# A gated cross-attention and MoE layer on one core: softmax maxima finished 12 half slots ahead, weighted sums at every slot's end

## The chip, the cores and the metric

The kernel runs on one core of a Trainium2 chip. The metric is the device time of one execution in microseconds (us). A core has five engines that run beside each other, each with its own program in order: PE (matmuls; PEld is its weight load), DVE (vector), ACT (activations), POOL (general purpose, also issues some DMAs) and SP (issues DMAs). They meet by semaphores only.

## The reference, cut to what matters

16 batches of 512 tokens with 256 channels, and a context of 1601 rows with 128 channels. Each batch goes through layer norm, causal self-attention and cross-attention with 16 heads of 16, a projection, a residual, and then a mixture of experts (32 experts, top 4) plus a shared expert:

```
q, k, v = heads(x @ Wq + bq), heads(x @ Wk + bk), heads(x @ Wv + bv)
att  = where(causal, q k^T * scale, -inf);  y  = softmax(att) v
attc = qc kc^T * scale;                     y += softmax(attc) vc      # 1601 context rows
x = x + tanh(g) * (y @ Wp + bp)
x = x + tanh(g2) * (top-4 experts(layernorm(x)) + shared expert)
```

A softmax needs the maximum of each row, or something near it, before the exponentials.

## The kernel before, in words

**Parts.** The attention program is written out as a prologue P, a first batch F, 14 middle batches M, a last batch L, and a remainder X (`plan`, `run` in each engine's program). Then come the experts (`build_experts`) and a merge. A batch of attention carries the next batch's loads, norm and q/k/v work, and the projection, router, shared expert and routing of the batch before it.

**Slots.** A batch has 68 slots (`SLOTS`), four quads of 17: quad g = 2*ch + v holds 4 heads, with 13 slots of 128 context rows ("cross") and 4 of 128 own rows ("self"). A slot has two half slots of two heads each, so a batch has 136 half slots, and a quad 34. PE's order in one slot is (`run` in `pe_program`): scores of pair 0, items of the first half slot, scores of pair 1, items of the second, and at one of four places the weighted sums of the slot before. ACT takes the exponential of each score tile (line 766) into `prob`, which has two buffers, one per slot; PE multiplies `prob` with the values into the one bank `outs` (line 576). In the four self slots POOL first clears what lies above the diagonal (`mask`, line 1165), and the sums wait for that.

**The ring.** Scores and items take turns in seven PSUM banks (`RB`, `ring`), strictly in order of PE's program (`Plan.claim`). PE waits before it writes a bank until its last reader has read it: ACT for scores, DVE for most items.

**Maxima.** The row maxima of a quad are taken from a separate, coarser product of 34 items (`max_items`): 8 `own`, 24 `cross`, 2 `rest`. Each has two score tiles that PE computes (lines 634, 643, 654 and 659) and DVE reduces (line 962). When all are in, DVE makes `whole` (line 968), PE turns the result (`shift`, line 667), ACT and DVE write its two bf16 rows into `mr`, and SP sends them by 4 DMAs into the operand rows of the scores (`stacks<-mr`, line 1427). Scores of the quad wait for these (`rowed`). Before the change a quad's maxima end 6 half slots ahead of its first scores (`early = 6`): `whole` at half slots 28, 62, 96 and 130.

**What sets the order.** For F and L a planner deals items at fixed places and fills maxima by costs (`deal`, `fill`), with the sums after the second half slot's items (place 3). For the 14 middle batches three tables do it: `PLACED` (half slot of each item by group), `MAXIMA` (number of maximum items in each half slot) and `SUMS_AT` (place of the sums in each slot: 0 after pair 0's scores, 1 after its items, 2 after pair 1's scores, 3 after its items). Of the items, these matter here:

- `finish_a`: the last batch's load of x (`xr`), `bias`, four `outproj`, `norm2`, two `trans`, `router`. After the last `outproj` DVE makes the statistics, POOL the inverse root in 16 small steps (`inverse_root`, lines 1152 to 1158, 4 rounds of 4), and DVE the normalised rows (`norm2`, line 888) that `trans` turns on PE. In POOL's program the second part of an item comes one half slot later, behind `mask` if that is a second half slot and ahead of it if it is a first.
- `split`: q, k and context projections in three bf16 pieces; `value`: the value projections; `stack`: SP's loads of operands, 12 DMAs each; SP stores a finished piece one half slot after it.
- `route`: the top-4 choice on DVE in 15 half slots from 77 on; `scatter`: 16 indirect DMAs of POOL. The first `split` of quad pair 1 waits on ACT until all 16 have landed (line 800).
- `divide` on POOL: products of 128x1024 and 128x512 (lines 1200 and 1204), at slots 7 and 41.

## Time and profile before

| | us |
|---|---|
| median of 3 runs | 4718.81 (4696.34 to 4723.49) |
| the profiled execution | 4715.91 |
| its span in the trace | 4713.8 |
| PE busy | 4143.5 (88%) |
| DVE busy | 3554.8 (75%) |
| ACT busy | 2678.1 (57%) |
| POOL busy | 1647.1 (35%) |

In the trace, L12 is line 12 of the kernel; `PE ring L552` is PE's instruction of that line that writes `ring`. A number in brackets behind a timeline row is the idle time of the engine before it, and what ended it. The profiled execution's time is 2.1 us more than its span, and lies 2.9 us under the median. PEclk (or the clock in a window) is the share of full speed that was granted to TensorE: it has two levels, 0.5 (1.2 GHz) and 1.0 (2.4 GHz), and a window shows their mean.

### The profile page before, as it was taken

The page shows a single profiled execution, that of the slowest core. Times are in us where ns is not written, and L with a number is a line of the kernel's source. Part 1 is how long each engine was busy: PE and PEld are TensorE (multiplying, and loading weights), DVE is VectorE, ACT ScalarE, POOL GpSimd, SP SyncE. Part 2 cuts the span into 40 slices and gives each one's busy share as a digit, 9 for nine tenths or more (in the row PEclk, how much of TensorE's full clock was granted, in tenths as well). Part 3 has the DMA queues.
Part 4 walks back from the last instruction along what each step waited for, and adds up shares of the span by engine and source line. Part 5 has one row for each costly group of instructions (what it writes and reads, how often), then busy time and mean ns, then how long its engine had stood idle before and what let it go on. Part 6 is the DMA issues. An engine that isn't in the chain of part 4 may idle for free. (4 is left out here: it accounts for less than half of the span.)

```text
span 4713.8 us, 87834 instructions
## 1 busy us (share of the span) xinstructions
PE 4143.5 (88%) x30693; PEld 1734.6 (37%) x30693; DVE 3554.8 (75%) x7733; ACT 2678.1 (57%) x5523; POOL 1647.1 (35%) x2168
## 2 busy tenths in 40 slices
PE   4999999999999999999999989999999995788882
PEld 1333333323333333333333333333333322577771
DVE  5888888888979797879797979787888873344442
ACT  1665656565656565656565666666665663444440
POOL 1122323232323232323232323223232313588883
PEclk7999999999999999999999999999999997899996
DMA  3333434343434343434343334343433335888888
GB/s 111 82 84 84 110 81 115 82 116 77 115 81 115 78 113 78 116 73 114 85 113 86 108 89 106 88 107 85 110 84 103 95 102 161 170 151 150 149 150 246
DMA packets 384060, 514.13 MB, mean 109 GB/s; under 512 B 84628, under 2 KB 248324, under 8 KB 383680
## 3 DMA queue, kind: packets, MB, share of 16 engines
q1 hardware_dynamic: 288720, 380.51, 30.5%
q0 software_dynamic: 87728, 115.39, 13.6%
q10 hardware_dynamic: 7232, 13.26, 0.9%
q8 instruction: 227, 3.72, 0.3%
q14 instruction: 153, 1.25, 0.1%
HBM read 288.49 MB, written 201.27 MB: 104 GB/s over the span
## 5 line engine op out<-in xcount | busy, mean ns | idle before, releaser
L766 ACT ACTIVATE prob<-ring 128x512 f32<-128x512 f32 (+3 forms) x4352 | 2132.9, 562 | 1185.2 <-PE ring L552 1153.3
L962 DVE TENSOR_REDUCE pmx<-ring 128x1 f32<-128x512 f32 (+1 forms) x3328 | 1992.0, 662 | 169.3 <-PE ring L634 153.2
L552 PE MATMUL ring<-stacks 64*128 64x512 bf16 (+1 forms) x8704 | 1308.3, 374 | 123.2 <-DMA stacks<-mr 56.1
L576 PE MATMUL outs<-prob,vt 128*32 128x512 f32 x8704 | 1106.3, 581 | 90.1 <-POOL prob L1165 88.3
L552 PEld LDWEIGHTS ring<-stacks 64*128 64x128 bf16 (+1 forms) x8704 | 331.9, 96 | 1169.3 <-issue 627.7
L634 PE MATMUL ring<-stacks 64*128 64x512 bf16 x3072 | 609.8, 394 | 16.2 <-DVE pmx L962 3.3
L962 DVE TENSOR_REDUCE mc<-ring 128x1 f32<-128x128 f32 (+3 forms) x1024 | 432.0, 482 | 243.6 <-PE ring L659 241.0
L1690 POOL DMA_INDIRECT scratch_sums<-e_yo,e_tok x320 | 495.9, 1550 | 117.3 <-issue 82.5
L1165 POOL TENSOR_SCALAR_AFFINE_SELECT prob<-prob 128x512 f32<-128x512 f32 x256 | 167.1, 653 | 1015.8 <-ACT prob L766 1013.7
L1235 POOL TENSOR_TENSOR split<-rest,split 128x512 bf16<-128x512 f32 (+1 forms) x224 | 218.9, 977 | 778.2 <-DVE split L1057 775.6
L1662 DVE TENSOR_SCALAR e_yo<-e_py,e_wcol 128x256 f32<-128x256 f32 x320 | 140.2, 480 | 286.8 <-DMA scratch_sums<-e_yo,e_tok 284.6
L576 PEld LDWEIGHTS outs<-prob,vt 128*32 128x32 f32 x8704 | 173.8, 109 | 472.5 <-issue 295.7
L634 PEld LDWEIGHTS ring<-stacks 64*128 64x128 bf16 x3072 | 177.4, 97 | 428.1 <-issue 130.3
L1564 PE MATMUL e_ph<-e_xt,e_we 128*128 128x256 f32 x1280 | 307.2, 383 | 3.4 <-ACT e_xt L1600 3.2
L1224 POOL DMA_INDIRECT scratch_slots<-split,rows x256 | 252.6, 987 | 92.6 <-issue 69.9
L800 ACT ACTIVATE split<-ring,bcol 128x512 bf16<-128x512 f32 (+1 forms) x224 | 142.1, 636 | 215.4 <-PE ring L603 124.3
L1609 ACT COPY e_we<-stacks 128x768 f32 x160 | 133.1, 832 | 230.9 <-issue 121.6
L1564 PEld LDWEIGHTS e_ph<-e_xt,e_we 128*128 128x128 f32 x1280 | 240.6, 191 | 45.3 <-ACT e_xt L1600 12.4
L1573 PE MATMUL e_py<-e_we,e_act 128*128 128x256 f32 x640 | 178.8, 402 | 61.5 <-DVE e_act L1646 59.5
L1054 DVE SCALAR_TENSOR_TENSOR rest<-ring,bcol,split 128x512 f32<-128x512 f32 (+1 forms) x224 | 150.9, 674 | 91.7 <-ACT split L800 91.7
L654 PE MATMUL ring<-stacks 64*128 64x128 bf16 (+3 forms) x1024 | 169.5, 331 | 46.8 <-DMA stacks<-scratch_parts 15.7
L1200 POOL TENSOR_TENSOR num<-num,den 128x1024 f32<-128x1024 f32 x31 | 73.3, 2365 | 228.7 <-DMA den<-scratch_inverses 223.1
(168 smaller groups left out, 3744.0 us busy)
## 6 DMA issues: line engine op xcount, KB each, us to landing
stacks<-scratch_parts SPq DMA_DIRECT2D x1536, 64.0 KB, 3.1
stacks<-scratch_parts SPq DMA_DIRECT2D x768, 68.1 KB, 2.6
scratch_parts<-split SPq DMA_DIRECT2D x64, 768.0 KB, 4.1
e_xin<-scratch_slots SPq DMA_DIRECT2D x160, 289.0 KB, 3.6
scratch_parts<-split SPq DMA_DIRECT2D x32, 816.8 KB, 4.3
num<-oc POOLq DMA_DIRECT2D x256, 64.0 KB
den<-scratch_inverses POOLq DMA_DIRECT2D x63, 256.0 KB, 7.7
ct<-in_ctx_t_dram SPq DMA_DIRECT2D x16, 800.5 KB, 5.2
```

The costliest lines, as they stand in the source:

```text
L552: mm = eng.matmul(dst[0:m, q0:T], kst[g][step][on, pair, k0:k0 + m], qst[g][step][on, pair, qc + q0:qc + T], start=step == 0, stop=step == 1)
L576: mm = eng.matmul(po[32 * j:32 * j + 32, q0:T], vt[ch][0:m, VW * vi + VE * hl:VW * vi + VE * hl + 32], prob[0:m, n % 2, j, q0:T], start=kt ...
L634: eng.matmul(dst, qst[g][0][on, pair, 128 * qt:128 * qt + 128], kst[g][0][on, pair, T + 512 * of:T + 512 * of + 512], start=True, stop=Tru ...
L654: eng.matmul(dsts[side][:, 0:n], qst[g][0][on, pair, T + 128 * qt:T + n], kst[g][0][on, pair, 0:n], start=True, stop=False)
L766: eng.activation(prob[0:m, n % 2, j, q0:T], pm[0:m, PLANS[part.kind].bank[i], q0:T], ACT.Exp, scale=SCALE).then_inc(exped.sem, 1)
L962: eng.tensor_reduce(dst, src, AX.X, ALU.max).then_inc(free_of(part, it, side), 1)
L1165: eng.affine_select(out=prob[:, n % 2, :, q0:q0 + 128], in_=prob[:, n % 2, :, q0:q0 + 128], compare_op=ALU.is_ge, fill=0.0, base=0, patter ...
L1224: eng.indirect_dma_start(scr["slots"], bass.IndirectOffsetOnAxis(ap=rows[:, NQ * k + q:NQ * k + q + 1].bitcast(U32), axis=0), xs[:, ROW * ...
L1235: eng.tensor_tensor(last, rest[:, no % 2, 0:n], mid, ALU.subtract).then_inc(low.sem, 1)
L1564: op = eng.matmul(phd[i][:, m, :], we[g % UW][:, c0:c0 + H], xt[i][:, kc, :], start=kc == 0, stop=kc == KC - 1)
L1573: op = eng.matmul(py[i][:, q, :], act[i][:, 128 * q:128 * q + 128], we[g % UW][:, 2 * KC * H:], start=True, stop=True)
L1690: eng.indirect_dma_start(scr[f"sums{i}"], bass.IndirectOffsetOnAxis(ap=tok[u][:, q:q + 1].bitcast(U32), axis=0), yo[g % UO][:, q, :], None ...
```

## The change

Maxima now end 12 half slots ahead of the quad's scores (`AHEAD`), so `whole` stands at half slots 22, 56, 90 and 124. The first 13 maximum items of quad 1 (8 `own`, 5 `cross`) move from a batch's start into the last 12 half slots of the batch before it (`NEXT`, items marked "next"); F does them for the first middle batch, and all 34 of its own besides; L has only the 21 that are left for quad 1. The sums stand at place 3 in every slot. The tables of the middle batches are others: with that, `outproj` moves from (26, 26, 30, 30) to (24, 26, 32, 32), `trans`, `trans`, `router` from (40, 40, 40) to (40, 42, 42), the scatters from one in each half slot from 96 on to (98, 99, 102, 102, 102, ... 111), and `stack` items go earlier. The route items stay where they were, the other places move by a few half slots. DVE's waits ahead of `whole` name the newest use of each bank instead of the quad's last items. No instruction of a middle batch is added or removed.

```diff
+AHEAD, NEXT = 12, 13
+
+
+def parted_items(q, which):
+
+    items, costs = max_items(q)
+    if which == "next":
+        return [it + ("next",) for it in items[:NEXT]], costs[:NEXT]
+    return (items[NEXT:], costs[NEXT:]) if which == "rest" else (items, costs)
+
...
 PLACED = {
-    "value1": (1, 6, 8, 8, 11),
-    "stack2": (12, 16, 20),
-    "stack3": (50, 54, 58),
-    "finish_a": (8, 24, 26, 26, 30, 30, 37, 40, 40, 40),
-    "finish_b": (44, 47),
-    "finish_c": (50, 50, 50, 51),
-    "next": (42, 54, 47, 53, 56, 56),
-    "split0": (57, 60, 62, 67, 69, 72, 73),
-    "value0": (93, 97, 100, 104, 108),
-    "split1": (114, 118, 119, 124, 126, 130, 131),
+    "value1": (2, 2, 8, 10, 10),
+    "stack2": (6, 10, 14),
+    "stack3": (44, 48, 52),
+    "finish_a": (8, 24, 24, 26, 32, 32, 37, 40, 42, 42),
+    "finish_b": (44, 45),
+    "finish_c": (50, 50, 50, 50),
+    "next": (42, 54, 47, 53, 54, 54),
+    "split0": (56, 60, 61, 67, 68, 70, 72),
+    "value0": (94, 100, 103, 107, 110),
+    "split1": (114, 118, 120, 124, 125, 128, 133),
     "route": (77, 78, 79, 80, 81, 82, 83, 84, 85, 86, 87, 89, 91, 92, 93),
-    "scatter": (96, 97, 98, 99, 100, 101, 102, 103, 104, 105, 106, 107, 108, 109, 110, 111),
-    "stack0": (84, 88, 92),
-    "stack1": (118, 122, 126),
+    "scatter": (98, 99, 102, 102, 102, 103, 105, 107, 107, 107, 108, 108, 108, 109, 111, 111),
+    "stack0": (78, 82, 86),
+    "stack1": (112, 116, 120),
 }
 MAXIMA = (
-    3, 2, 2, 1, 0, 1, 1, 2, 1, 1, 1, 2, 1, 1, 0, 1, 2, 1, 1, 1, 0, 2, 1, 1, 1, 2, 0, 2, 2, 1, 2, 0, 0, 1,
-    1, 2, 0, 0, 0, 1, 1, 2, 0, 1, 2, 1, 0, 2, 1, 2, 0, 2, 1, 0, 1, 1, 1, 2, 1, 2, 0, 1, 4, 1, 3, 0, 3, 0,
-    0, 3, 0, 2, 1, 0, 2, 1, 2, 1, 2, 0, 0, 0, 0, 0, 0, 1, 0, 0, 0, 3, 0, 1, 0, 0, 1, 3, 0, 0, 2, 1, 1, 1,
-    1, 2, 0, 1, 0, 1, 2, 1, 1, 1, 0, 1, 2, 1, 1, 1, 2, 2, 0, 1, 1, 2, 0, 0, 2, 0, 1, 2, 0, 0, 0, 0, 0, 0,
+    0, 0, 1, 2, 0, 1, 1, 1, 1, 2, 2, 2, 1, 1, 0, 2, 0, 1, 0, 2, 0, 1, 1, 0, 2, 2, 2, 2, 0, 1, 0, 1, 1, 0,
+    0, 2, 0, 0, 0, 0, 2, 1, 2, 2, 2, 2, 0, 1, 0, 1, 2, 1, 0, 1, 1, 2, 4, 1, 2, 2, 3, 1, 1, 1, 0, 1, 1, 2,
+    1, 1, 1, 1, 1, 1, 1, 1, 1, 1, 1, 0, 0, 0, 0, 0, 0, 1, 0, 0, 0, 3, 1, 1, 0, 1, 2, 2, 1, 1, 0, 1, 1, 1,
+    0, 2, 0, 1, 1, 0, 1, 1, 2, 2, 1, 1, 2, 1, 0, 1, 2, 1, 1, 1, 0, 1, 2, 1, 1, 1, 2, 0, 1, 2, 0, 1, 1, 1,
 )
 SUMS_AT = (
-    1, 1, 3, 3, 3, 1, 2, 3, 1, 3, 3, 3, 2, 3, 3, 2, 3, 0, 3, 3, 3, 3, 3, 0, 2, 3, 2, 2, 3, 2, 2, 2, 2, 1,
-    1, 2, 3, 2, 3, 1, 3, 3, 3, 1, 1, 1, 3, 2, 0, 3, 1, 2, 2, 3, 3, 2, 3, 3, 2, 1, 3, 2, 3, 2, 2, 2, 2, 2,
+    3, 3, 3, 3, 3, 3, 3, 3, 3, 3, 3, 3, 3, 3, 3, 3, 3, 3, 3, 3, 3, 3, 3, 3, 3, 3, 3, 3, 3, 3, 3, 3, 3, 3,
+    3, 3, 3, 3, 3, 3, 3, 3, 3, 3, 3, 3, 3, 3, 3, 3, 3, 3, 3, 3, 3, 3, 3, 3, 3, 3, 3, 3, 3, 3, 3, 3, 3, 3,
 )
 
 
...
                 i += 1
 
     fin, more = kind in "ML", kind in "FM"
-    quad, early = HALF // 2, 6
+    quad = HALF // 2
     deal("value1", 0, (3, 5, 7, 9, 11), value_items(1), 1.35)
-    deal("stack2", 0, (12, 16, 20), stack_items(2), 0.0)
-    deal("stack3", 0, (50, 54, 58), stack_items(3), 0.0)
+    deal("stack2", 0, (6, 10, 14), stack_items(2), 0.0)
+    deal("stack3", 0, (44, 48, 52), stack_items(3), 0.0)
     if fin:
         deal("finish_a", 0, (8, 24, 27, 27, 31, 31, 37, 39, 39, 41), FINISH[:10], 0.9)
         deal("finish_b", 0, (43, 45), FINISH[10:12], 2.9)
...
     if kind == "L":
         deal("experts", 0, (36, 70, 104), [("experts", i) for i in range(3)], 0.0)
     if more:
-        deal("stack0", 0, (84, 88, 92), stack_items(0), 0.0)
-        deal("stack1", 0, (118, 122, 126), stack_items(1), 0.0)
-    at = 0
-    for q in range(1, 5 if more else 4):
-        fill(at, quad * q - early, *max_items(q % 4))
-        at = quad * q - early
-        out[at].append(("whole", q % 4))
-        out[at + 1].append(("shift", q % 4))
+        deal("stack0", 0, (78, 82, 86), stack_items(0), 0.0)
+        deal("stack1", 0, (112, 116, 120), stack_items(1), 0.0)
+    stages = [(1, 0, quad - AHEAD, "rest" if fin else "all")]
+    stages += [(q % 4, quad * (q - 1) - AHEAD, quad * q - AHEAD, "all") for q in range(2, 5 if more else 4)]
+    if more:
+        stages.append((1, 2 * HALF - AHEAD, 2 * HALF, "next"))
+    for g, lo, hi, which in stages:
+        fill(lo, hi, *parted_items(g, which))
+        if which != "next":
+            out[hi].append(("whole", g))
+            out[hi + 1].append(("shift", g))
 
     first = {2 * n + p // 2 for n in range(SLOTS) for p in (0, 2) if sums_at(kind, n) == p}
...
+        def newest_of(part, g):
+
+            p = PLANS[part.kind]
+            mine = [it for here in p.items for it in here if it[0] in ("own", "cross", "rest") and it[1] == g and it[-1] != "next"]
+            return {p.bank[it, i]: p.turn[it, i] for it in mine for i in range(BANKS[it[0]])}
...
-        load_no = lambda part, g: 1 if part.kind == "P" else (1, 0, 1, 1)[g]
+        load_no = lambda part, it: 1 if part.kind == "P" or it[-1] == "next" else (1, 0, 1, 1)[it[1]]
...
-                    pe.wait_ge(stacked_rest[g], part, load_no(part, g))
+                    g, pair, qt, of = it[1:5]
+                    pe.wait_ge(stacked_rest[g], part, load_no(part, it))
...
-                    newest = {bank_of(part, it, i): (it, i) for it in max_items(g)[0] for i in range(BANKS[it[0]])}
-                    for last, i in newest.values():
-                        read(dve, part, last, i)
+                    for k in range(RB):
+                        dve.wait_ge(freed[k], part, newest_of(part, g).get(k, 0))
                     eng.tensor_reduce(mc[g % 2][:, :].rearrange("p (h a q) -> p h a q", a=2, q=NQ)[:, :, 0, :], pmx[:, :, :, :],
                                       AX.X, ALU.max).then_inc(whole.sem, 1)
```

## Rows read from the trace of the kernel before

**Rows 1.** The page, part 1: busy time, share of the span, instructions
```profile
PE 4143.5 (88%) x30693; PEld 1734.6 (37%) x30693; DVE 3554.8 (75%) x7733; ACT 2678.1 (57%) x5523; POOL 1647.1 (35%) x2168
```

**Rows 2.** Windows: first, middle, last batches, two single ones; length, busy, clock, DMA
```profile
116.23:335.08 218.85, 208.52 (x1670) 70.07 (x1672) 179.03 (x365) 145.09 (x301) 44.86 (x72) 0.98 0.35 84
335.08:3711.99 3376.91, 3125.03 (x24618) 1130.25 (x24615) 2837.14 (x6020) 2085.84 (x4271) 1008.28 (x1596) 0.96 0.38 97
3711.99:3924.00 212.01, 196.15 (x1548) 64.54 (x1548) 141.40 (x301) 137.65 (x286) 54.30 (x83) 0.95 0.39 105
...
577.73:820.50 242.77, 224.97 (x1764) 80.78 (x1762) 202.81 (x430) 149.07 (x305) 71.92 (x114) 0.95 0.38 96
1304.22:1542.19 237.97, 219.45 (x1763) 79.96 (x1761) 202.41 (x430) 148.95 (x306) 72.12 (x114) 0.98 0.38 98
```

**Rows 3.** Waits of PE, middle batch 1304.2:1542.2: total us, times, longest
```profile
PE outs L576 <- POOL prob L1165: 6.0, 3, 5.0
PE ring L552 <- DMA stacks<-mr: 3.8, 1, 3.8
PE ring L552 <- DVE pmx L962: 3.5, 4, 2.6
PE ring L682 <- ACT xt L789: 1.0, 1, 1.0
```

**Rows 4.** Timeline of PE around slot 16
```profile
1357.29 0.61 PE L552 MATMUL ring<-stacks 64*128 64x512 bf16 x4
1362.93 0.65 PE L576 MATMUL outs<-prob,vt 128*32 128x128 f32 x8 [5.03 <-POOL prob L1165]
```

**Rows 5.** Timeline of POOL there, first root step and mask
```profile
1357.90 0.20 POOL L1152 TENSOR_TENSOR newt<-rstd 128x4 f32<-128x4 f32 x1 [1.24 <-DVE rstd L882]
...
1362.24 0.63 POOL L1165 TENSOR_SCALAR_AFFINE_SELECT prob<-prob 128x512 f32<-128x512 f32 x1
```

**Rows 6.** Timeline of DVE, statistics and normalisation of the same batch
```profile
1355.59 1.40 DVE L874 BATCH_NORM_STATS2 stat<-ct 128x6 f32<-128x256 f32 x4
...
1368.05 1.38 DVE L888 TENSOR_SCALAR xa<-ct,mv,rstd 128x256 f32<-128x256 f32 x4
```

**Rows 7.** Timeline of PE and SP at the batch's end
```profile
1536.49 3.36 SPq L1427 DMA_DIRECT2D stacks<-mr  x4
...
1541.14 1.21 PE L552 MATMUL ring<-stacks 64*128 64x512 bf16 x4 [3.82 <-DMA stacks<-mr]
```

**Rows 8.** Windows at three spots of another middle batch (columns as in rows 2)
```profile
635.50:642.30 6.80, 6.04 (x42) 2.10 (x42) 4.34 (x9) 3.60 (x7) 2.75 (x6) 0.50 0.09 10
...
649.10:655.90 6.80, 6.80 (x35) 2.03 (x38) 2.80 (x6) 2.39 (x5) 0.00 (x0) 0.50 0.89 174
...
816.40:823.20 6.80, 3.72 (x34) 2.06 (x36) 2.09 (x6) 1.08 (x2) 0.00 (x0) 0.50 0.20 72
```

**Rows 9.** Timeline of DVE and POOL in slots 40 to 42
```profile
1453.87 2.45 POOL L1200 TENSOR_TENSOR num<-num,den 128x1024 f32<-128x1024 f32 x1 [8.30 <-DMA den<-scratch_inverses]
1454.13 2.33 DVE L998 TENSOR_TENSOR split<-split,down 128x128 f32<-128x128 f32 x1
...
1458.83 0.29 DVE L998 TENSOR_TENSOR split<-split,down 128x128 f32<-128x128 f32 x1
```

**Rows 10.** Timeline of POOL and ACT, slots 47 to 57, first and last of sixteen scatters
```profile
1476.05 1.08 POOL L1224 DMA_INDIRECT scratch_slots<-split,rows  x1 [0.18 <-issue]
...
1502.21 0.97 POOL L1224 DMA_INDIRECT scratch_slots<-split,rows  x1 [0.30 <-issue]
...
1505.27 0.69 ACT L800 ACTIVATE split<-ring,bcol 128x512 bf16<-128x512 f32 x1 [2.40 <-DMA scratch_slots<-split,rows]
```

**Rows 11.** Timeline of PE in the last batch, where slots are bare
```profile
3906.21 1.06 PE L576 MATMUL outs<-prob,vt 128*32 128x512 f32 x8
...
3908.18 1.06 PE L576 MATMUL outs<-prob,vt 128*32 128x512 f32 x8
```

**Rows 12.** Groups by form, whole span: the reduction of one score tile
```profile
L962 DVE TENSOR_REDUCE pmx<-ring 128x1 f32<-128x512 f32 x3072 | 1904.8, 682 | 156.1 <-PE ring L634 153.2
```

More of the change, by code:

```diff
@@ L628, in item @@
                 elif what == "cross":
-                    g, pair, qt, of = it[1:]
-                    pe.wait_ge(stacked_rest[g], part, load_no(part, g))
+                    g, pair, qt, of = it[1:5]
+                    pe.wait_ge(stacked_rest[g], part, load_no(part, it))
                     for side in range(2):
@@ L636, in item @@
                 elif what == "rest":
-                    g, pair = it[1:]
-                    pe.wait_ge(stacked_rest[g], part, load_no(part, g))
+                    g, pair = it[1:3]
+                    pe.wait_ge(stacked_rest[g], part, load_no(part, it))
                     dsts = [take(part, it, side) for side in range(2)]
@@ L647, in item @@
                 elif what == "own":
-                    g, pair, qt = it[1:]
+                    g, pair, qt = it[1:4]
                     n = 128 * (qt + 1)
-                    pe.wait_ge(stacked[g], part, load_no(part, g))
+                    pe.wait_ge(stacked[g], part, load_no(part, it))
                     dsts = [take(part, it, side) for side in range(2)]
```

## The prediction

> **What bounds the kernel now.** I read the page first: PE is busy for 88% of the span, DVE for 75% [rows 1]. A share over the whole span hides the stages, so the windows came next, cut where the first exponential of each batch starts. The 14 middle batches take 3376.91 us, 241.2 each, of 4713.8; in the undisturbed one PE is busy for 219.45 of 237.97 us and DVE for 202.41 [rows 2]. So PE is the bound of a middle batch, with 18.5 us in which it does nothing, and DVE is close behind. What ends these idle times the view of waits tells: 6.0 us mask on POOL, 3.8 us operand rows by DMA, 3.5 us ring banks held by DVE, 1.0 us the rows' transpose copied by ACT [rows 3]; the rest is in many small ones.
>
> Three of them are single places, seen in the timeline. (1) Slot 16, the last self slot of quad 0: PE stands for 5.03 us until POOL has masked [rows 4]. The mask starts at 1362.24, and in front of it stand 16 small steps of the inverse root, from 1357.90 on [rows 5]. ACT had its exponentials long before. (2) The batch's end: PE waits 3.82 us for the rows of the next quad, whose DMAs were issued only at 1536.49 [rows 7]. (3) Slots 40 to 44, where DVE makes the routing and PE runs out of banks, 2.6 us at the longest [rows 3].
>
> The granted clock is the fourth thing. Behind (1) and (2) it is at 0.50, in some batches twice behind (1) [rows 8]. A batch at a mean clock of 0.95 took 242.77 us, one at 0.98 took 237.97 [rows 2]. As the clock has the levels 0.5 and 1, that is 2 x 0.05 x 242.8 = 24.3 us at the low one against 9.5, so one us at the low clock costs 4.8/14.8 = 0.32 us.
>
> **The change part by part, for one middle batch.**
>
> The projections. The last two go from half slot 30 to 32. POOL makes the inverse root one half slot later, so now behind the mask of slot 16 and not ahead of it. The 16 steps stay, in front of nothing that PE waits for: -5.0 us [rows 4, 5]. What is late next is the normalisation. From the first statistics to the end of the root it is 1362.24 - 1355.59 = 6.7 us, and 1.4 us for the rows: 8.1 us [rows 5, 6]. On PE's side, from the same point to the transpose in half slot 40, stand about 6.3 us: the last self half slot, six half slots of 0.98 (a bare slot, scores and sums, takes 3908.18 - 3906.21 = 1.97 us [rows 11]), and four maximum items in them and ahead of the transpose; the statistics start some 0.7 us after the projection, which is taken off. PE then waits 8.1 - 6.3 = +1.8 us. Bounds 0 (DVE's other work and the masks slow PE as well) and 3.
>
> The rows of quad 0. `whole` and `shift` go from half slots 130/131 to 124/125, and SP gets the four DMAs behind the store of one split piece instead of behind the last. Between them and the first score that needs them now lie 10 half slots, over 10 us, against 3.4 us of issue and the landing [rows 7]. The wait goes, 3.8 us, and of two short ones just ahead of it, in the bare self slots, half a microsecond: -4.3. SP also issues the `stack` loads 4 to 6 half slots earlier; all of them are 8 or more half slots ahead of their first reader, and I cost them at 0. If that cover were gone, PE would wait for the landing in each quad, some 3 us a time.
>
> Thirteen items to the batch's end. They cost PE and DVE the same there as at the start. DVE: 5 cross items of 2 x 0.682 us [rows 12] and 8 own ones, some 14.5 us in all, now lie in half slots that had no maximum work. PE and DVE have the same sum as before, spread over 136 half slots and not 130. 0, bounds -2 and +3.
>
> The routing stretch. DVE is close to the bound from half slot 68 to 90, where (3) lies. The table takes 14 items down to 11 in half slots 68 to 78, and 5 to 3 in the last three of them, right ahead of the routing; two items are 2.7 us less backlog on DVE [rows 12], which could take away all of (3). But POOL's `divide` still falls on the routing: DVE's product took 2.33 us beside it and 0.29 a little later [rows 9]. And `whole` and `shift` of quad 3 now stand in half slots 90 and 91, right behind three maximum items and the rank: PE has to stand at the shift until DVE has caught up, some 1.5 us. Together -1.0, bounds -3.5 and +3.
>
> Here a rule of the Trainium skill (SBUF — State Buffer, section "SBUF: two separate sides") speaks against the change: a DVE instruction with two SBUF inputs and a GpSimd one share a port pair that is locked for a whole instruction. By that the trace's 2.33 us against 0.29 is a lock, and it stays whatever the tables do to the maxima, since neither instruction moves.
>
> The scatters. All 16 take from 1476.05 to 1503.18 us, POOL without a pause but for masks and its other DMAs, and ACT's first split waits 2.40 us for the last to land [rows 10], almost without cost, as PE has a projection of 2 us to do. Now they start two half slots later and pause for the mask of slot 50: 14 of them start at half slot 102. At 0.97 + 0.30 us each [rows 10], with some 3.4 us of POOL's other DMAs (what is left of the 26.2 us between first and last, less masks and pauses), that is 21 us, for some 18.5 us until half slot 114. ACT waits 2 to 3 us longer, and behind ACT the ring fills: +2.0, bounds 0 and +4.
>
> The sums at the slot's end. They are further behind the exponentials and masks they wait for, so that no wait can grow on that side. The exponentials of the next slot need the buffer that these sums free, and PE computes those scores only after the sums in any case. On the other side up to four banks of items come at one time: +0.5. First and last batch run with place 3 now, and a bare slot of the last one is full with 0.97 + 1.00 us of PE work [rows 11].
>
> The clock. A mean of 0.96 is 2 x 0.04 x 241.2 = 19.3 us a batch at the low level [rows 2], three quarters of them behind (1) and (2) by the lengths in rows 8 and the batches like it. 15 us x 0.32 = -5.0, bounds -1.5 (new stalls bring it back) and -7. By a rule of the Trainium skill (TensorE: Matmul & The Clock Gate, section "Terms") time at the low clock costs half of itself, which would be -7.5 and some 35 us less in the sum; the two batches of rows 2 say 0.32, part of that time being idle anyway.
>
> Sum: -5.0 + 1.8 - 4.3 - 1.0 + 2.0 + 0.5 - 5.0 = -11.0 us a batch, 14 times: -154. The first batch gets 13 items more (DVE 14.5 us, PE some 3) and loses a wait of some 2 at its end: +3, bounds 0 and +13. The last has 13 fewer: -6, bounds -3 and -14. The experts behind it, 789.8 us with everything else, don't change. In all -157: 4715.9 (the profiled execution) - 157 = 4559 us. That execution lies 2.9 us under the median; the difference is left out.
>
> **The rivals.**
>
> A, the forecast: waits (1) and (2) go, little comes in their place, 4559. For it: both waits are in every middle batch, and the order of the programs takes their cause away.
>
> B, DVE becomes the bound. It is busy for 202 us of 238 [rows 2], and 227 would be left. Where maxima lie one in each half slot, a slot needs 4 x 0.682 = 2.7 us of DVE and 2.4 of PE. Then half of the gain is lost in ring waits: -5.5 x 14 - 3, 4636. For it: rows 12. Against: DVE's own idle times (1) and (2) go as well.
>
> C, new waits eat it up: transpose +3, shift +3, scatters +4, each at its upper bound, and each long enough to bring the low clock back (-1.5 in place of -5.0): -11.0 + 1.2 + 4 + 2 + 3.5 = -0.3 a batch, 4709. Against: three ends at once.
>
> D, slower: the sums at the slot's end. Four banks of items and four of scores are more than the seven of the ring, so in slots with two pairs of items PE stops for DVE ahead of the sums, and the sums can't be put in between as the old table did in 38 of 68 slots. The price is at most one reduction, 0.68 us; it decides the sign where 38 x 0.29 us eat the 11 us a batch, and at 0.45 it is 17.1: 6.1 x 14 - 3 = +82, 4798. Against: rows 11, and in the last batch, which has place 3 throughout, nothing of the kind.
>
> E, the change doesn't do what it says: the root is late for another reason, or rows wait for something else than the order, and only one of the two waits and its clock goes: -80, 4636. Against: rows 5 and 7 show both causes.
>
> **How the numbers follow.** A 0.62, B 0.16, E 0.08, C 0.09, D 0.05. The sums of the terms' ends would be wider; they don't fall together. A's own range is 4490 to 4610; the range goes on to B and E, and leaves out C and D and what is under 4480: 4480 to 4670. A measurement of this kernel tells about 1%, 47 us, from no change. Faster by over 1%: A, B, E and a little of C, 0.87. Within 1%: most of C, 0.08. Slower: D, 0.05.
>
> **What would show it.** Right: in the waits of PE no mask wait over 1 us and no wait for the rows by DMA in a middle batch; the root's 16 steps on POOL behind slot 16's mask; middle batches of 228 to 232 us; a mean clock of 0.98 or more; PE idle for 8 to 12 us. Then, one by one: a wait of PE for DVE's normalised rows at the transpose of some 1.8 us, ACT's wait for the scatters at 4 to 5 us, a short wait at the shift in half slot 91. B shows as DVE busy for over 93% of a middle batch and PE's waits for `pmx` above 8 us; C as three waits of over 3 us with the low clock behind each; D as more waits for the ring in front of the sums over the whole batch. I am wrong in the main if the middle batches are still over 238 us.

## The result, and the profile after

The changed kernel takes 4588.35 us, the median of 4 runs (4572.39 to 4595.78), beside 4714.85 us of the kernel before: ratio 0.973, 95% interval 0.969 to 0.977, so 2.7% faster. The forecast was 4559 us, a gain of 157; the gain is 126. The profiled execution took 4589.19 us with a span of 4587.2.

The page of the changed kernel, part 1, columns as in [rows 1]:

```profile
PE 4120.5 (90%) x30693; PEld 1738.2 (38%) x30693; DVE 3527.5 (77%) x7733; ACT 2655.2 (58%) x5523; POOL 1647.9 (36%) x2168
```

There are as many instructions as before, and no engine works less by more than 28 us. Most of the gain is idle time of PE. Windows of the changed kernel: first batch, the 14 middle ones, everything from the last batch on, and one middle batch (columns as in [rows 2]):

```profile
115.79:340.47 224.68, 212.31 (x1722) 72.72 (x1722) 190.43 (x389) 146.02 (x300) 44.95 (x72) 0.99 0.33 82
340.47:3590.97 3250.50, 3102.72 (x24614) 1133.34 (x24615) 2811.01 (x6023) 2063.14 (x4271) 1007.27 (x1596) 0.97 0.40 101
3590.97:4587.20 996.23, 747.24 (x4153) 509.24 (x4149) 462.69 (x1195) 434.73 (x934) 577.53 (x450) 0.90 0.75 155
1271.45:1503.86 232.41, 221.50 (x1760) 80.89 (x1758) 200.38 (x430) 147.37 (x305) 72.02 (x114) 0.97 0.39 101
```

A middle batch takes 3250.50/14 = 232.2 us, 9.0 less than in [rows 2]. PE's busy time, taken from the length, leaves 10.6 us without work in a batch, where [rows 2] have (3376.91 - 3125.03)/14 = 18.0: 7.4 of the 9.0 us. The other 1.6 are busy time, which fits that less of it runs at the low clock (below). The first batch is 5.8 us longer, all that follows the middle batches 5.6 shorter than the 1001.81 before. With 0.4 at the start, -126.4 + 5.8 - 5.6 - 0.4 = -126.6 is the difference of the spans.

The waits of PE in that middle batch (total us, times, longest):

```profile
PE ring L572 <- DVE rest L1073: 2.4, 1, 2.4
PE ring L737 <- DVE split L1027: 2.4, 1, 2.4
PE ring L654 <- DVE pmx L982: 1.3, 4, 0.7
PE ring L572 <- issue: 0.9, 1, 0.9
PE ring L608 <- DVE xa L908: 0.9, 1, 0.9
PE ring L702 <- ACT xt L809: 0.8, 1, 0.8
```

The mask and the rows by DMA, first and second in [rows 3], are gone, and `pmx` is down to small pieces. Of the new waits the longest are a split's `rest` and the rank product (line 737), the count of each expert's rows; a smaller one is for the normalised rows `xa`. Over all middle batches the rank's wait is 2.6 us in the mean and that for `rest` 1.8.

The new wait at the rank, in the timeline of POOL, DVE and PE at half slot 89:

```profile
1417.71 2.34 POOL L1219 TENSOR_TENSOR num<-num,den 128x1024 f32<-128x1024 f32 x1 [9.81 <-DMA den<-scratch_inverses]
...
1418.27 1.94 DVE L1016 TENSOR_TENSOR split<-split 128x128 f32<-128x128 f32 x1
...
1420.24 1.31 DVE L1017 TENSOR_TENSOR split<-split,down 128x128 f32<-128x128 f32 x1
...
1422.93 0.18 PE L737 MATMUL ring<-split,tri 128*128 128x32 bf16 x1 [2.38 <-DVE split L1027]
```

Two small products of DVE (0.29 us each when alone, [rows 9]) take 1.94 and 1.31 us beside POOL's two large ones (the second runs from 1420.13 to 1421.40), 2.7 us more than they need, and PE waits 2.4 for the choice that hangs on them.

POOL's large product has moved, though its place in the program has not: in the middle batches of the kernel before it starts in half slot 81 or 82, and in those of the changed one in 87 to 89. What it waits for is the load of `den`, which comes later. First the load's row before the change (its product is in [rows 9]), then the changed kernel's store and load:

```profile
1444.91 0.66 POOL L1193 DMA_DIRECT2D den<-scratch_inverses  x1 [1.13 <-DMA scratch_inverses<-dsum]
```

```profile
1403.94 0.59 POOL L1206 DMA_DIRECT2D scratch_inverses<-dsum  x1 [1.37 <-DVE dsum L914]
...
1407.26 0.65 POOL L1212 DMA_DIRECT2D den<-scratch_inverses  x1 [2.72 <-DMA scratch_inverses<-dsum]
```

The load takes 8.6 us from issue to landing before and 11.3 in the changed kernel, in the mean of the 14 batches, and is issued 15.0 and 10.1 us ahead of half slot 87. SP's `stack0` loads now stand at half slots 78, 82 and 86, where the inverses travel; whether they are what slows them was not tried.

The new wait behind the scatters, in the same batch:

```profile
1462.28 0.96 POOL L1243 DMA_INDIRECT scratch_slots<-split,rows  x1 [0.30 <-issue]
...
1465.74 0.69 ACT L820 ACTIVATE split<-ring,bcol 128x512 bf16<-128x512 f32 x1 [4.44 <-DMA scratch_slots<-split,rows]
...
1466.46 0.75 DVE L1073 SCALAR_TENSOR_TENSOR rest<-ring,bcol,split 128x512 f32<-128x512 f32 x1 [3.54 <-ACT split L820]
...
1467.27 1.03 PE L572 MATMUL ring<-stacks 64*128 64x512 bf16 x4 [2.41 <-DVE rest L1073]
```

ACT's wait of 2.40 us in [rows 10] is now 4.44 (3.8 in the mean of the 14 batches), DVE waits behind ACT, the ring fills and PE stands for 2.41.

The clock was read in windows at three spots of that batch: behind the wait for `xt`, at the rank, and behind the scatters.

```profile
1337.31:1340.72 3.41, 3.41 (x24) 0.89 (x22) 2.25 (x5) 1.09 (x2) 0.00 (x0) 0.50 1.02 245
1422.64:1426.05 3.41, 3.12 (x26) 0.95 (x28) 3.41 (x8) 0.00 (x0) 0.00 (x0) 0.50 0.68 157
1467.02:1473.85 6.83, 6.58 (x24) 1.80 (x25) 4.63 (x9) 3.49 (x7) 1.08 (x1) 0.50 0.07 20
```

So waits of 2.4 us, and a chain of waits of 0.9, 0.65 and 0.8, have the low level behind them as those of 5.0 and 3.8 had [rows 8]. The table sums the clock records of all middle batches: us at the low level per batch, each low spell counted in the stretch of half slots in which it begins.

| half slots | 0-23 | 24-36 | 37-46 | 47-67 | 68-97 | 98-118 | 119-135 | batch |
|---|---|---|---|---|---|---|---|---|
| before | 0.2 | 6.3 | 3.2 | 0 | 4.9 | 0 | 6.3 | 21.0 |
| changed | 0.5 | 0 | 4.6 | 0 | 4.9 | 3.7 | 0 | 13.7 |

Both stretches whose waits the change removed run at full clock, 12.6 us less at the low level. 5.1 come back in two others: 1.4 in half slots 37 to 46, and 3.7 behind the scatters. Around the rank nothing changes: 4.9 us before, behind PE's waits for ring banks, and 4.9 now; PE's waits in half slots 68 to 97 are 3.6 us a batch before and 3.5 now.

### The profile page after: what moved, and what is told of

Read it like the earlier page. It is cut to its first block and busy times, and to the rows that moved or that the text cites. A ratio compares the mean times of both kernels' runs of the same rounds, so it can differ in the third digit from the quotient of the medians.

```text
span 4587.2 us, 87838 instructions
## 1 busy us (share of the span) xinstructions
PE 4120.5 (90%) x30693; PEld 1738.2 (38%) x30693; DVE 3527.5 (77%) x7733; ACT 2655.2 (58%) x5523; POOL 1647.9 (36%) x2168
## 5 line engine op out<-in xcount | busy, mean ns | idle before, releaser
L572 PE MATMUL ring<-stacks 64*128 64x512 bf16 (+1 forms) x8704 | 1241.3, 369 | 48.4 <-DVE rest L1073 25.4
L596 PE MATMUL outs<-prob,vt 128*32 128x512 f32 x8704 | 1119.7, 587 | 7.2 <-POOL prob L1184 6.7
L572 PEld LDWEIGHTS ring<-stacks 64*128 64x128 bf16 (+1 forms) x8704 | 312.9, 96 | 1236.4 <-issue 627.6
L654 PE MATMUL ring<-stacks 64*128 64x512 bf16 x3072 | 653.4, 390 | 29.7 <-DVE pmx L982 23.9
L654 PEld LDWEIGHTS ring<-stacks 64*128 64x128 bf16 x3072 | 190.7, 96 | 352.3 <-DVE pmx L982 143.7
L1583 PEld LDWEIGHTS e_ph<-e_xt,e_we 128*128 128x128 f32 x1280 | 240.7, 191 | 45.3 <-ACT e_xt L1619 12.6
L674 PE MATMUL ring<-stacks 64*128 64x128 bf16 (+3 forms) x1024 | 150.2, 303 | 29.9 <-DMA stacks<-scratch_parts 16.1
```

The costliest lines, as they stand in the source:

```text
L572: mm = eng.matmul(dst[0:m, q0:T], kst[g][step][on, pair, k0:k0 + m], qst[g][step][on, pair, qc + q0:qc + T], start=step == 0, stop=step == 1)
L596: mm = eng.matmul(po[32 * j:32 * j + 32, q0:T], vt[ch][0:m, VW * vi + VE * hl:VW * vi + VE * hl + 32], prob[0:m, n % 2, j, q0:T], start=kt ...
L654: eng.matmul(dst, qst[g][0][on, pair, 128 * qt:128 * qt + 128], kst[g][0][on, pair, T + 512 * of:T + 512 * of + 512], start=True, stop=Tru ...
L1583: op = eng.matmul(phd[i][:, m, :], we[g % UW][:, c0:c0 + H], xt[i][:, kc, :], start=kc == 0, stop=kc == KC - 1)
```

## The experiments

Four variants take one part out of, or put one part into, a kernel; four move one item of the changed kernel; the last four follow up. Chips differ. e1 to e8 ran on one where the kernel before takes 4783 to 4794 us, e11 and e12 on another (4792), e9 and e10 on one where it takes 4707. The chip of the result isn't named on record; the kernel before took 4715 us there, and here it is counted with that of e9 and e10 as the first, by its time and its traces; the others are the second and third. So ratios, each to the kernel before on its own chip, are what is compared. The changed kernel lies at 0.973 on the first and 0.974 on the second.

**e1: the projections alone, in the kernel before.**

```diff
-    "finish_a": (8, 24, 26, 26, 30, 30, 37, 40, 40, 40),
+    "finish_a": (8, 24, 26, 26, 32, 32, 37, 40, 40, 40),
```

> The kernel before, with the last two projections at half slot 32 in place of 30; nothing else. Theory W (the gain is two waits of PE and the low clock behind them): the 5.0 us mask wait of slot 16 goes, some 0.9 us at the transpose come, the low clock behind it shrinks: -4.5 to -6 us in each of 14 batches, so -65 to -80 us, ratio 0.983 to 0.986. Rival S (the evener spread of maxima and sums over the half slots makes the gain, no single wait): under -20 us, ratio 0.996 or more.

4716.93 us, ratio 0.987 (0.984 to 0.989). PE's mask waits fall from 82.5 us in the 14 batches, 5.0 at the longest, to 7, and the transposes get no wait. Outside the scatters' stretch (half slots 98 to 118, see e5) a batch is 5.4 us shorter than in the trace of before (201.4 for 206.8), taken on the other chip. Two entries of one table moved by two half slots give half of the whole gain, as theory W expected; rival S is out for this half.

**e2: the places of the sums alone, in the kernel before.**

```diff
-SUMS_AT = (1, 1, 3, 3, 3, 1, 2, 3, ...)
+SUMS_AT = (3, 3, 3, 3, 3, 3, 3, 3, ...)
```

> The kernel before, with the weighted sums at place 3 in all 68 slots; nothing else. Theory W: the sums' place is no bound, within 15 us of before (ratio 0.997 to 1.003); the mask wait stays at 5 us or gets shorter by what PE does ahead of it, below 1 us. Rival S: faster by 30 us or more. Rival D of the prediction (sums at the end cost ring waits): slower by 40 us or more.

4836.84 us, ratio 1.011 (1.009 to 1.013): some 54 us slower, 3.8 a batch. Theory W's "within 15 us" failed; rival D had the sign and the size right for this part taken alone. The waits of PE in the 14 middle batches of e2:

```profile
PE outs L576 <- POOL prob L1165: 57.6, 28, 3.4
PE ring L552 <- DMA stacks<-mr: 53.0, 14, 4.6
PE ring L552 <- DVE pmx L962: 46.9, 44, 3.1
PE ring L682 <- ACT xt L789: 13.8, 14, 1.0
PE ring L654 <- issue: 13.5, 14, 1.0
PE ring L634 <- issue: 10.8, 8, 1.7
PE ring L654 <- ACT prob L766: 8.9, 14, 0.7
PE ring L634 <- ACT prob L766: 8.7, 7, 1.7
```

The mask wait even shrinks (5.9 to 4.1 us a batch), since the sums come later; against it stand new waits of the items on lines 634 and 654, for banks that ACT frees and for what the profile shows no cause of.

**e3: the projections of the changed kernel back at half slot 30.**

```diff
-    "finish_a": (8, 24, 24, 26, 32, 32, 37, 40, 42, 42),
+    "finish_a": (8, 24, 24, 26, 30, 30, 37, 40, 42, 42),
```

> The kernel after, with the last two projections back at half slot 30. Theory W: the mask wait of about 5 us comes back behind slot 16, +5 us and a spell of the low clock in each of 14 batches: +60 to +90 us on the kernel after, ratio to before 0.986 to 0.993. Rival S: within 15 us of the kernel after, ratio 0.970 to 0.976.

4696.12 us, ratio 0.982 (0.980 to 0.984): 0.8% slower than the changed kernel, some 37 us by the ratios and 25 by the medians (the kernel before takes 4783 us beside e3 and 4794 beside e5). Theory W's 60 to 90 failed, and so did rival S's 15. Waits of PE, 14 middle batches of e3:

```profile
PE outs L596 <- POOL prob L1184: 16.8, 14, 2.0
```

It is 1.2 us a batch in place of 5.9. The sums' place alone takes it to 4.1 (e2), so the other tables cover most of the mask's lateness; which of them wasn't told apart. The wait for the normalised rows (0.9) is gone too. The two edits overlap, so the gains of e1 and of the rest can't be added.

**e4: the sums' old places in the changed kernel.**

```diff
-SUMS_AT = (3, 3, 3, 3, 3, 3, 3, 3, ...)
+SUMS_AT = (1, 1, 3, 3, 3, 1, 2, 3, ...)
```

> The kernel after, with the places of the sums of the kernel before (38 of 68 slots not at the end). Theory W: within 20 us of the kernel after (ratio to before 0.969 to 0.978), short mask waits of up to 0.5 us come back in the self slots. Rival S: half of the gain or more goes, ratio above 0.985.

4906.23 us, ratio 1.026 (1.024 to 1.028), 5.3% slower than the changed kernel and slower than the kernel before. Theory W's "within 20 us" failed. PE's waits, 14 middle batches:

```profile
PE ring L572 <- issue: 64.1, 43, 3.1
PE ring L654 <- DVE pmx L982: 39.6, 96, 3.1
PE ring L572 <- DVE rest L1073: 33.9, 28, 1.5
PE ring L572 <- DVE pmx L982: 17.2, 78, 0.8
```

The places also set whether maxima or whole-array items come first in a half slot (`first` in `plan`), so the old places turn that order around under the new tables, and the run can't tell the two effects apart. Each of the two sets of tables is slower with the other's places.

**e5: the changed kernel on the second chip.**

> The kernel after, unchanged, on the chip of the runs beside it, as the base for them. The ratio to before is that of the first comparison, 0.969 to 0.977, and batches' stretches read against e6 to e8: 2.6 us of PE's wait for DVE at the rank in half slot 89, 1.8 us for DVE behind the scatters in half slot 115, 2.5 us in three waits in half slots 40 to 42.

4671.24 us, ratio 0.974 (0.972 to 0.976). Here the first chip's trace and the second's can be laid side by side. Half slots 98 to 118 of the same batch, first the result's trace, then e5's, each a view of windows:

```profile
1437.90:1475.78 37.88, 35.35 (x256) 12.64 (x252) 29.68 (x59) 21.55 (x45) 22.30 (x27) 0.91 0.39 110
```

```profile
1464.14:1505.61 41.47, 37.30 (x256) 12.73 (x252) 29.88 (x59) 21.88 (x46) 22.29 (x27) 0.92 0.35 100
```

Over all middle batches this stretch takes 36.2 and 41.3 us, and all the rest 196.0 and 196.4. Of the 5.5 us by which a middle batch differs between the chips, 5.1 lie in the stretch of the sixteen indirect DMAs. It seems to be there without the change too: 34.4 us before on the first chip, 39.5 in e1 on the second, where no trace of the kernel before itself was taken.

**e6: POOL's division of quad 1 at slot 46 instead of 41.**

```diff
-                    g = ended(part, n, 8)
-                    if g is not None and g % 2:
-                        divide(part, g)
+                    for behind, late in ((8, False), (13, True)):
+                        g = ended(part, n, behind)
+                        if g is not None and g % 2 and (g == 1) == late:
+                            divide(part, g)
```

> The kernel after, with POOL's divide of the first quad pair at slot 46 (behind the routing) in place of slot 41. Theory L (DVE and POOL lock each other out, and that is what makes PE wait at the rank): DVE's products in slots 40 to 42 take 0.3 us each, the 2.6 us wait at the rank and the low clock behind it go, 3 to 4 us a batch, -40 to -55 us on e5, ratio 0.011 lower. Rival (DVE's routing chain is too long for PE in any case): the products get short, but the wait stays above 1.5 us and the time within 15 us of e5.

4667.45 us, ratio 0.974 (0.972 to 0.976): nothing, and the rank still waits in 12 of 14 batches. But the edit did not do what it was made for. POOL has nothing that it must wait for between the two slots, and the product starts when the copies of the inverses land by DMA, wherever it stands in the program. What the theory asks can be read from the batches in which the product comes late by itself. One such batch of e6:

```profile
1440.93 2.35 POOL L1219 TENSOR_TENSOR num<-num,den 128x1024 f32<-128x1024 f32 x1 [12.07 <-PE ring L663]
...
1441.02 0.19 PE L737 MATMUL ring<-split,tri 128*128 128x32 bf16 x1
...
1446.42 0.23 PE L674 MATMUL ring<-stacks 64*128 64x128 bf16 x2 [3.35 <-DMA stacks<-scratch_parts]
```

(The row names PE's line 663 as the releaser; by the program the product waits for the DMAs into `num` and `den` alone.) Here DVE was done with the choice before POOL began, and the rank waits for nothing. In the eight traces of changed tables with the sums at the slot's end and the rank at half slot 89 (112 middle batches) POOL's product overlaps the choice in 100, and the rank waits 1.8 to 2.9 us in each; in the 12 others it waits in none. So there wait and overlap come and go together; e4, with the sums' old places, has the overlap too and waits of 0.1 to 1.2. It doesn't follow that its end is a gain: in each of these 12 the operand loads come late as well, PE waits 3.2 to 4.6 us for them a little further on, and half slots 87 to 91 take 13.4 us in the mean, beside 12.3 in the 100.

**e7: the scatters back at half slots 96 to 111.**

```diff
-    "scatter": (98, 99, 102, 102, 102, 103, 105, 107, 107, 107, 108, 108, 108, 109, 111, 111),
+    "scatter": (96, 97, 98, 99, 100, 101, 102, 103, 104, 105, 106, 107, 108, 109, 110, 111),
```

> The kernel after, with the 16 scatters in half slots 96 to 111 as before. Theory W (the later scatters make ACT's split, then DVE and PE wait in half slots 114 and 115): the 1.8 us wait of PE and the low clock behind it go, ACT's wait is 2.4 us again, -25 to -40 us on e5; mask waits of up to 0.5 us in the self slots may come back. Rival (the wait comes of the split itself): within 10 us of e5.

4617.79 us, ratio 0.964 (0.962 to 0.966): 53 us under e5, more than the 25 to 40 expected, and faster than both kernels. The same stretch as in e5, windows of e7:

```profile
1442.12:1480.31 38.19, 36.48 (x256) 12.69 (x252) 30.06 (x59) 21.70 (x45) 21.31 (x26) 0.91 0.37 104
```

Over all middle batches it takes 38.2 us where e5 has 41.3, PE's wait for `rest` is gone, and the low clock falls from 17.1 to 11.0 us a batch.

**e8: transposes, router and hidden products two or one half slots later.**

```diff
-    "finish_a": (8, 24, 24, 26, 32, 32, 37, 40, 42, 42),
-    "finish_b": (44, 45),
+    "finish_a": (8, 24, 24, 26, 32, 32, 37, 42, 44, 44),
+    "finish_b": (45, 46),
...
-    "next": (42, 54, 47, 53, 54, 54),
+    "next": (44, 54, 47, 53, 54, 54),
```

> The kernel after, with the two transposes of the normalised rows at half slots 42 and 44, the router at 44, the hidden products at 45 and 46 and the load of x at 44: PE comes to them when the rows are ready. Theory W: the 0.9 us wait for DVE's rows and the 0.8 us for ring banks go, and most of the low clock in half slots 41 to 43 with them, -15 to -35 us on e5. Rival (the low clock there comes of the small matmuls of transposes and router, not of the waits): below -12 us, the low spells stay.

4708.14 us, ratio 0.982 (0.980 to 0.984): 37 us slower than e5, not 15 to 35 faster, which neither theory foresaw. The wait for `xa` is gone, and the maxima wait instead (14 middle batches of e8; e5 has 22.7):

```profile
PE ring L654 <- DVE pmx L982: 41.1, 77, 1.6
```

**e9 and e10: e7 with the rank at half slot 91; and with the divide of e6 and the router at 43 besides.**

```diff
-    "route": (77, 78, 79, 80, 81, 82, 83, 84, 85, 86, 87, 89, 91, 92, 93),
+    "route": (77, 78, 79, 80, 81, 82, 83, 84, 85, 86, 87, 91, 92, 93, 94),
```

> The changed kernel with the sixteen row stores at half slots 96 to 111 as in e7, and with the count product (rank) at half slot 91 instead of 89, and what follows it (pick, rows_a, rows_b) at 92, 93 and 94 instead of 91, 92 and 93. Theory C (a short wait of TensorE costs its length and the low clock that comes behind it): the rank wait of 2.20 us a batch goes and the low spell of 3.4 to 6.8 us (mean about 4) at half slots 89 and 90 goes with it, which at 0.32 us lost per us at the low clock is another 1.3 us; 3.5 us a batch, 49 us in all, ratio to the kernel before 0.953 to 0.955, low time per middle batch 7 us instead of 11.0. Theory W (only the wait's length counts, the clock falls anyway somewhere near): 2.2 us a batch, 31 us, ratio 0.957 to 0.958, low time still 11. Rival M (the wait moves to the pick or to the first store, whose row numbers now come one half slot later, or VectorE is late with the maxima around 91): within 10 us of e7, ratio 0.962 to 0.966, with a new wait of over 1.5 us between half slots 91 and 98.

> e9 and two edits more: GpSimd's divide of quad 1 at the end of slot 46 instead of 41 (e6), and the router product at half slot 43 instead of 42, one half slot behind the second transpose. Theory C: against e9 another 0.45 us a batch from the divide and 0.8 us of the wait for the transposed array, with about 2 us of low clock (0.6 us): 1.5 to 1.9 us a batch, 20 to 27 us, ratio about 0.949 (0.946 to 0.951), and half slot 42 at 3.0 to 3.6 us instead of 4.4 with 43 longer by 0.5 or less. Rival (as in e8: the router then stands next to the two hidden products of 2.9 us, ScalarE has no room between them and the maxima wait): no better than e9, or slower by 5 to 20 us, with half slots 43 to 45 longer by over 1 us together than they lose at 42.

4553.24 us and 4555.51, ratios 0.967 (0.965 to 0.968) and 0.967 (0.966 to 0.969). The rank waits no more, and PE stands for the maxima in the same place. DVE and PE in e9:

```profile
1418.37 2.37 DVE L1017 TENSOR_TENSOR split<-split,down 128x128 f32<-128x128 f32 x1
...
1422.59 3.16 DVE L982 TENSOR_REDUCE pmx<-ring 128x1 f32<-128x512 f32 x6
...
1423.33 1.03 PE L572 MATMUL ring<-stacks 64*128 64x512 bf16 x3 [1.70 <-DVE pmx L982]
```

DVE's reductions wait behind the same slow products, and the ring holds PE at the next scores. Low time is 12.9 us a batch, not 7. Rival M is right: the wait has only moved, though to half slots 89 and 90 and not behind 91. So theories C and W fail as forecasts, and what a wait costs in clock stays untested here, since no wait was taken away. Half slots 98 to 118 take 33.2 us here, windows of e9 in the same batch as above:

```profile
1438.64:1471.69 33.05, 32.63 (x256) 12.10 (x252) 29.52 (x59) 21.50 (x45) 21.26 (x26) 1.00 0.39 111
```

That is 3.0 us less than the changed kernel on this chip (36.2), at full clock; on the second chip e7 gained 3.1 there. So the scatters' new places cost some 3 us a batch on both chips, the rank's edit in e9 being taken as without effect so far behind it.

**e11 and e12: e7 once more; and with the divide of e6, the first transpose at 41 and the router at 43.**

```diff
-    "finish_a": (8, 24, 24, 26, 32, 32, 37, 40, 42, 42),
+    "finish_a": (8, 24, 24, 26, 32, 32, 37, 41, 42, 43),
```

> The kernel of e7 once more (only the sixteen row stores back at half slots 96 to 111), to compare it on one chip with e9 and e10. On the chip of e3 to e8 it lay at 0.964 of the kernel before; e9, whose only further edit is the rank product two half slots later, lay at 0.967 on another chip. Theory C of e9 (the rank wait and the low clock behind it cost 3.5 us a batch) wants e7 slower than e9: 4590 to 4605 us where the kernel before takes 4707, ratio 0.975 to 0.978. Rival M (moving the rank only moved the wait: e9 has 4.0 us a batch of waits for the maxima at half slots 89 to 91 where the changed kernel had 2.0) wants e7 equal or faster: 4530 to 4555 us, ratio 0.962 to 0.9675, with the rank wait of 2.2 us still there.

> e7 with the divide of quad 1 at slot 46 (e6), the first transpose at half slot 41 instead of 40 and the router product at 43 instead of 42. Theory C: the wait for the normalised array (0.9 us) goes, and the wait for the transposed array (0.8 us) shrinks as in e10, with half of the low clock of half slots 41 and 42 (some 2 us a batch, 0.6 us): against e11 1.5 to 2.3 us a batch, 21 to 32 us, ratio lower by 0.0045 to 0.007. Rival (as in e8 and e10: TensorE only runs sooner into the wait for the maxima at half slots 41 to 44, because VectorE normalises there): within 8 us of e11, with the waits for the maxima longer by as much as the others are shorter.

4624.36 us and 4625.95, ratios 0.964 (0.963 to 0.966) and 0.966 (0.964 to 0.967). e11 repeats e7 on a third chip. e12 is its rival's case: the waits for `xa` and `xt` (0.9 and 0.8 us a batch) are gone, and the waits for `pmx` on line 654 grow from 20.0 to 29.2 us in the 14 batches, with a new one in front of the `rest` items (14 middle batches of e12):

```profile
PE ring L654 <- DVE pmx L982: 29.2, 47, 1.6
...
PE ring L663 <- DVE pmx L982: 10.5, 14, 0.9
```

The best version is e7: 0.964 on two chips, 1% under the change itself. On the first chip it was not run alone; e9, which differs from it by the rank only, lies at 0.967 there. Whether the rank's later place costs that 0.3% or the chip does isn't settled; outside the scatters' stretch e9's batch is 197.4 us and those of e7 and e11 195.0 and 196.3.

## Why the prediction was right, and what was off

The case was A: both single waits go and little comes in their place, and PE stays the bound. By its own terms, per middle batch:

- **The projections (-5.0).** Right. The mask waits are gone, and e1, which has this edit alone, is 5.4 us a batch shorter outside the scatters, some clock included. The normalised rows were to be late by 1.8 us; the changed kernel shows 0.9. Why it is half isn't shown: it isn't the sums' place, since e4 with the old places shows 0.9 too. It runs as was worked out: last mask at 1320.87, root from 1323.08 to 1327.48, rows behind it.

```profile
1320.87 0.64 POOL L1184 TENSOR_SCALAR_AFFINE_SELECT prob<-prob 128x512 f32<-128x512 f32 x1 [2.51 <-ACT prob L786]
...
1323.08 0.20 POOL L1171 TENSOR_TENSOR newt<-rstd 128x4 f32<-128x4 f32 x1 [1.57 <-DVE rstd L902]
...
1327.52 1.44 DVE L908 TENSOR_SCALAR xa<-ct,mv,rstd 128x256 f32<-128x256 f32 x4 [2.14 <-POOL rstd L1177]
...
1329.10 0.63 PE L608 MATMUL ring<-ident,xa 128*128 128x128 f32 x4 [0.91 <-DVE xa L908]
```

- **The rows of quad 0 (-4.3).** Right by its wait, 3.7 us in the mean: SP issues them at 1489.77, 14 us ahead of the next batch, and no wait for them is left. In half slots 119 to 135 PE's waits fall by 3.1 us a batch (4.7 to 1.5), as new short ones stand there now, 0.9 us the longest. That part wasn't tried alone; the tables would have to be drawn up anew.

```profile
1489.77 2.62 SPq L1446 DMA_DIRECT2D stacks<-mr  x4
```

- **The routing stretch (-1.0, with a wait of 1.5 at the shift).** Half right. The maxima's waits shrank (4.3 us a batch before, 2.0 after), and one of 2.6 came, but at the rank in half slot 89 and not at the shift in 91; within half slots 68 to 97 PE's waits stay at 3.5 us. The prediction had the overlap of POOL's product with DVE's in its rows and left it out of the sum, "since neither instruction moves". That reading was wrong: the product starts 1.3 us behind the start of half slot 87 in the mean and not 6.2 ahead of it, beside the last step of the choice and not an earlier one. The rule of the Trainium skill (SBUF — State Buffer, section "SBUF: two separate sides"), a port pair locked for a whole instruction, agrees with 1.94 and 1.31 us beside 0.29 and with the 100 and 12 batches told under e6. Whether the lock costs more now than before isn't shown: moving what waits for it gained nothing in e9, and no run moved the product itself.
- **The scatters (+2.0, ACT's wait at 4 to 5 us).** Right in mechanism, somewhat small: ACT waits 3.8 us in the mean, 4.4 at the longest, PE waits 1.8 for `rest`, in half slots 98 to 118 only 0.4 more than before in all (1.5 to 1.9), and by e7 and e9 the places cost some 3 us a batch with the clock.
- **The sums (+0.5).** As a term it can't be had: +3.8 alone in the kernel before (e2), -16.5 in the changed one (middle batches of e5 against e4). That the sum is hardly touched by this is luck; it was wrong to price this edit by itself.
- **The clock (-5.0).** This is the step that failed. 15 of 19.3 us at the low level were to go; 7.3 of 21.0 went. It failed in two parts. Behind waits (1) and (2) stood 12.6 of 21.0 us and not three quarters; the rest was behind the wait for `xt` (3.2) and the ring waits of the routing (4.9), and it stayed. And the new waits were priced at their own length only: 1.8 us a batch behind the scatters brought 3.7 us of low clock, and the waits of under 1 us around half slot 41 another 1.4. The rate itself held between before and changed: 0.32 x 7.3 = 2.3 in place of 5.0, which with 6.8 us less of waits gives 9.1, beside 9.0 measured. The four kernels traced on the first chip (before, changed, e9, e10) have middle batches of 241.2, 232.2, 230.6 and 230.0 us, and 218.4 us + PE's waits of over 0.15 us + 0.28 for each us at the low level gives each within 0.2 us. That is a fit with two free numbers to four kernels and no test; on the second and third chips the same sum is 1.4 to 8.0 us short. By the rule of the Trainium skill (TensorE: Matmul & The Clock Gate, section "Terms"), half of the low time, it would be 3.7, and 6.8 of idle time with that 10.5 us, where 9.0 were measured.
- **First and last batch.** +5.8 for +3, -5.6 for -6.

In sum, PE's waits of over 0.15 us are 6.8 us a batch less, forecast 6.0, and the clock gave 2.3 for 5.0: 9.0 for 11.0 a batch, 126 for 154 in the middle batches. That the waits came so close is partly luck. By the stretches of the table above they changed by -5.0 (half slots 24 to 36), +1.5, -0.4, -0.1, +0.4 and -3.1 (119 to 135) us a batch: routing and rows gave some 1 us less each than forecast, and the scatters' waits took 1.6 less. The middle batches at 232.2 us just miss the 228 to 232 that was to show the forecast right, the clock at 0.97 the 0.98. B doesn't show (`pmx` 2.0 us a batch, DVE busy 86% of a middle batch), nor C's three waits of over 3 us.

## What to carry to other kernels

When a wait is taken away, list which waits the new order makes, and give each not only its length but also the low clock behind it: here a wait of 1.8 us a batch and some of under 1 us took back 5.1 of the 12.6 us that the change had freed from the low level. Tables that are written out by hand work as a set (e2 and e4), so a part of such an edit can be slower than the kernels at both its ends, and single terms don't add. And an instruction moved in an engine's program has moved in time only if something it must wait for lies between the two places (e6): check that on the timeline before a theory is given up on its account. The reverse holds as well: POOL's product kept its place in the program and moved by some six half slots, since the DMA it waits for did.

## What the runs showed of the hardware that was not expected

The chips differ by 1.5 to 1.8% with the same kernel, and 5.1 of the 5.5 us by which a middle batch differs lie where POOL issues sixteen indirect DMAs, with the scatters themselves as long (median 0.97 us on either chip). In e5 ACT and DVE stand there, up to 4.7 and 2.4 us at a time, for matmuls whose recorded end is long past: the semaphore that the matmul gives rises only when they start. One such wait of ACT ends at 536.59, and its semaphore rises at 536.57 to 536.60; the matmul had ended at 534.1. The view calls what ended such a wait "remote". Waits in the 14 middle batches of e5, of which the first chip's traces show none:

```profile
ACT prob L786 <- remote: 65.3, 27, 4.7
DVE pmx L982 <- remote: 37.7, 22, 2.4
```

Semaphores of PE that rose over 0.7 us behind the recorded end of their matmul are there in each of the ten traces from the second and third chips, before ACT or DVE 71 to 167 times in the middle batches and always in half slots 99 to 113. The four traces from the first chip have none. The ends of matmuls are modelled in the profile, so the matmuls may have run late as well as their signals. What holds them up stays open, since no run told it apart.
